# Decoder layer on one core: the splits of the experts' weights, all placed in front of the last routing

## The chip, the cores and the metric

One core of a Trainium2 chip runs the whole program in one launch. The metric is the device time of one execution in microseconds (us); less is better. The engines are TensorE (PE), VectorE (DVE), ScalarE (ACT), GpSimd (POOL) and SyncE (SP), which only issues transfers here.

## The reference

x has 8 sequences of 256 tokens with 512 channels, in float32. Three blocks follow one another, each behind a layer norm and added to its input:

```python
x = x + _L0_attn_ref(_layernorm(x), w_qkv, w_out)          # causal self attention, 16 heads of 32
x = x + _L0_xattn_ref(_layernorm(x), mask, ctx, ctx, wq, wk, wv, wo)
                                    # one head of 512; keys and values: 256 rows of ctx, and 256 made from x
x = x + _L0_ffn_ref(_layernorm(x), wg, W, b)
...
logits = xt @ wg                                           # 8 experts
probs = softmax(logits); idx = argmax(probs); gate = probs[idx]
out = onehot(idx) * gate applied to (einsum('nh,eoh->neo', xt, W) + b)
```

Each token goes to its best expert alone, a 512 x 512 matrix with a bias, and the result is weighted with its probability.

## The kernel before

The program has three stages, each a block of its own with one instruction stream for each engine; at the end of a block the engines meet (line 946 is that of the second block). `self_attention` is the first stage. `cross_attention` is the second, and `mixture_of_experts` the third. Tokens are worked on in batches of 256 (B = 8), as two tiles of 128.

**Split products.** Every float32 product is made of three passes over rounded halves (`three_pass`, L60): a matrix is kept as a high part (rounded to float32r) and a low part (the rest). For activations ACT writes the high part (L1120) and DVE subtracts it from the source to get the low part (L1281).

**The experts' weights** are split in the same way, by `ExpertWeights` (L900 to L929). All eight stay in `w_hi` and `w_lo` of [128, 4, 8 x 512]; a matrix is 128 partitions x 2048 columns, 1 MB. The steps of one expert e are: `load` (SP) brings it into one of three staging buffers, e modulo 3, once the expert that was there has been split; `high` (ACT, L918) copies it rounded; `low` (GpSimd or DVE, L923) subtracts, over all 2048 columns in one instruction. Before the experts move in, the same places of `w_hi` and `w_lo` hold the weights and working matrices of the cross attention: q, k and v in the places of experts 0, 1 and 2, keys in 3, xt and qt in 4, values in 5, wo in 6, pt and ot in 7. An expert can be split only when its place is no longer in use: 0 to 2 once the q, k and v products of the last batch are done (v1 of batch 6), the others during or behind the last batch.

**The second stage** works through jobs, in one order on all engines:

```python
ORDER = ("X0 X1 s0 s1 q0 q1 p0 p1 q2 q3 o0 o1 o2 o3 k0 y0 y1 k1 k2 k3 v0 Y0 Y1 v1 l0 l1").split()
```

X transposes the normed tokens, q, k, v make queries, keys and values, s the scores, p transposes the probabilities, o multiplies with the values, y with wo, Y transposes the tokens normed for the third stage, l makes the logits. q, k, v and X are made a batch ahead, so the last batch runs only LAST: s0 s1 p0 p1 o0 to o3 y0 y1 Y0 Y1 l0 l1. Behind y1, DVE takes the statistics of x2 (L1256, L1260, b_veps in L1262), GpSimd raises to the power -1/2 (`rstd_ln3`, L1085), DVE writes xn_sb (L1266), TensorE transposes it (Y), DVE copies to xt3 (L1314), TensorE makes logits (L1237), DVE copies them (L1318).

**The routing** of a batch is done while the next one runs; that of the last batch stands at the head of the third stage. `choose` (DVE, L831 to L847: r_lmax, r_diff, r_eq, r_best, r_onehot, and the gate, with the exponential on ACT, L851), `count` (TensorE, L857 to L860), `place_tokens` (DVE, L869 to L877). Then `store_entries` (GpSimd, L884) scatters token numbers and gates into the table `slots` in memory, two indirect transfers of 128 entries, and `next_tokens` (GpSimd, L890, L893) waits until they have landed and writes the next token numbers, for which the next `choose` waits.

GpSimd's end of the second stage reads, before: `rstd_ln3(6)`, `store_entries(5)`, `next_tokens(5)`, lows of experts 1 and 2, `store_entries(6)`, low of 4, `rstd_ln3(7)`, `next_tokens(6)`. DVE makes the low part of 0 ahead of the last batch and that of 3 behind o3. ACT makes the high parts 0, 1, 2 ahead of the last batch and 3, 4, 5 behind it. In the third stage GpSimd makes the low part of 5 behind the last `store_entries`, ACT the high parts of 6 and 7, and DVE their low parts, ahead of its first product. The bias (16 KB, broadcast to 128 partitions, 2 MB) goes into `bias_sb`, whose first half holds wo raw until wo has been split.

**The third stage** takes 23 blocks of 128 tokens sorted by expert: SP reads 128 entries of `slots`, GpSimd gathers the rows (into the staging buffers, once the last expert of each has been split), TensorE transposes and multiplies (L1556, L60), DVE adds bias and residual, GpSimd scatters the result. TensorE starts when all experts are split and the owners of the blocks are known; c_at_i (L1613) is what SP needs to find a block's entries.

Of the kernel before, what the change touches and what calls it, by code (L numbers as in the profile page):

```python
# [10 lines left out]
F32 = mybir.dt.float32  # L11
# [9 lines left out]
P = 128  # L21
# [7 lines left out]
E = 8  # L29
# [866 lines left out]
class ExpertWeights:  # L896
# [1 line left out]

    def __init__(self, nc, cx, stage, loaded):
        sb = lambda n: cx.enter_context(nc.sbuf_tensor(n, [P, DC, E * D], F32R))
        sem = lambda n: cx.enter_context(nc.semaphore("e_" + n))
        self.hi, self.lo, self.stage, self.loaded = sb("w_hi"), sb("w_lo"), stage, loaded
        self.hi_done = sem("hi_done")
        self.split = [sem(f"split{i}") for i in range(STAGED)]

    def place(self, e, start=0, stop=D):
        return [t[:, :, e * D + start:e * D + stop] for t in (self.hi, self.lo)]

    def load(self, sp, w, e):
        wait(sp, self.split[e % STAGED], e // STAGED)
        sp.dma_start(self.stage[e % STAGED][:], w[e].rearrange("(c p) n -> p c n", p=P))\
            .then_inc(self.loaded[e % STAGED], 16)

    def high(self, nc, act, e):
        act.wait_ge(self.loaded[e % STAGED], 16 * (e // STAGED + 1))
        nc.scalar.copy(self.place(e)[0], self.stage[e % STAGED][:]).then_inc(self.hi_done, 1)  # L918

    def low(self, engine, e):  # L920
        hi, lo = self.place(e)
        engine.wait_ge(self.hi_done, e + 1)
        engine.tensor_tensor(lo, self.stage[e % STAGED][:], hi.bitcast(F32), ALU.subtract)\  # L923
            .then_inc(self.split[e % STAGED], 1)

    def all_split(self, engine):
        for i in range(STAGED):
            engine.wait_ge(self.split[i], len(range(i, E, STAGED)))


def cross_attention(nc, ident, routing, x1, x1_out, x1_last_out, ctx, ctx_t, wo, wg,
# [14 lines left out]
    with ExitStack() as cx:  # L946
# [78 lines left out]
        @block.sync  # L1025
        def _(sp):
            chunks = lambda t: t.rearrange("(c p) n -> p c n", p=P)
            channels = lambda b: ctx_t[b * D:(b + 1) * D, :] if isinstance(b, int) else ctx_t[bass.ds(b * D, D), :]
            load_ctx_t = lambda b: sp.dma_start(cin_t[:], chunks(channels(b))).then_inc(ct_in, 16)
            sp.wait_ge(unused_done, 2)  # L1030
            sp.dma_start(routing.table.rearrange("(p k) c -> p k c", p=P), unused[:]).then_inc(init_in, 16)
            load_ctx_t(1)
            sp.dma_start(wo_raw, chunks(wo)).then_inc(wo_in, 16)
            sp.dma_start(cin[:], batch_rows(ctx, 1)).then_inc(c_in, 16)
            sp.wait_ge(x1_out, 16 * (B - 1))
            sp.dma_start(xin[:], batch_rows(x1, 2)).then_inc(x_in, 16)
# [3 lines left out]
            for i in range(STAGED):  # L1040
                experts.load(sp, w, i)

            sp.wait_ge(wo_split, 2)
            sp.dma_start(bias_sb[:], bass.AP(tensor=bias.tensor, offset=bias.offset, ap=[[0, P], [1, E * D]]))\
                .then_inc(bias_in, 16)

            def batch(n, more, load):

                if load:
                    if not (isinstance(n, int) and n == 0):  # L1050
                        sp.wait_ge(xn_ready, n * TB)
                        sp.dma_start(xin[:], batch_rows(x1, n + 2)).then_inc(x_in, 16)
                    sp.wait_ge(ct_split, n + 1)
                    load_ctx_t(n + 2)
                    sp.wait_ge(c_split, n + 1)
                    sp.dma_start(cin[:], batch_rows(ctx, n + 2)).then_inc(c_in, 16)
                if not more:
                    for e in range(STAGED, E - 1):
                        experts.load(sp, w, e)
                sp.wait_ge(job_ev, ev_at("y1", n))  # L1060
                sp.dma_start(batch_rows(x2n[:, 0:D], n), x2_sb[:]).then_inc(x2_out, 16)
                if more:
                    sp.dma_start(xr[:], batch_rows(x1, n + 1)).then_inc(xr_in, 16)
                sp.wait_ge(xn3_ready, (n + 1) * TB)
                sp.dma_start(batch_rows(x2n[:, D:], n), xn3_sb[:]).then_inc(xn3_out, 16)

            batch(0, True, True)
            with sp.Fori(1, B - 2) as n:
                batch(n, True, True)
            batch(B - 2, True, False)  # L1070
            batch(B - 1, False, False)
            experts.load(sp, w, E - 1)

        @block.gpsimd
        def _(pool):
# [28 lines left out]
                routing.next_tokens(nc, pool, tick_pool, n - 1)  # L1104
            rstd_ln3(B - 2)
            routing.store_entries(nc, pool, tick_pool, B - 3)
            routing.next_tokens(nc, pool, tick_pool, B - 3)
            for e in (1, 2):
                experts.low(nc.gpsimd, e)
            routing.store_entries(nc, pool, tick_pool, B - 2)  # L1110
            experts.low(nc.gpsimd, 4)
            rstd_ln3(B - 1)
            routing.next_tokens(nc, pool, tick_pool, B - 2)

        @block.scalar
        def _(act):
# [15 lines left out]
            def batch(n):  # L1132
                for j in order(n):
                    if j[0] == "s":
                        q = int(j[1])
                        act.wait_ge(mx_done, n * TB + q + 1)
                        nc.scalar.activation(prob[:, q, :], bank(j, n)[:, :], ACT.Exp, scale=scale,
                                             bias=nmax[:, q:q + 1], accum_out=rsum[:, q:q + 1]).then_inc(ex_done, 1)
                    if j == "s1" and order(n) is ORDER:
                        ctx_t_hi(n + 1)  # L1140
                    if j in hi_jobs(order(n)):
                        hi_part(j, n)
                    if j == route_after(n) and has_routing(n):
# [9 lines left out]
            for e in range(STAGED):  # L1153
                experts.high(nc, act, e)
            batch(B - 1)
            for e in (3, 4, 5):
                experts.high(nc, act, e)

        @block.tensor
        def _(pe):  # L1160
# [87 lines left out]
                batch(n)  # L1248
            batch(B - 1)

        @block.vector
        def _(dve):
            def norm_stats(which, k, src, done):
# [39 lines left out]
            def batch(n):  # L1293
                for j in order(n):
# [33 lines left out]
                        ctx_t_lo(n + 1)  # L1328
                    if j == "o3" and order(n) is ORDER:
                        ctx_lo(n + 1)  # L1330
                    if j == "o3" and order(n) is LAST:
                        experts.low(nc.vector, 3)
                    if j == "p1":
                        nc.vector.reciprocal(rinv[:], rsum[:]).then_inc(rinv_done, 1)
                    if j == "y1":
# [20 lines left out]
def mixture_of_experts(nc, ident, routing, x2n, x2n_out, w, bias_sb, bias_in, out, stage, experts):  # L1356
# [17 lines left out]
    with ExitStack() as cx:  # L1374
# [35 lines left out]
        def rows(k, columns):  # L1410


            place, part = divmod(k % RX, RX // STAGED)
            first_column = part * 2 * D
            return stage[(E + place) % STAGED][:].rearrange("p c n -> p (c n)")[:, first_column + columns.start:
                                                                               first_column + columns.stop]


# [43 lines left out]
        def _(pool):  # L1462
# [9 lines left out]
            nc.gpsimd.tensor_copy(first[:], first_i[:]).then_inc(consts, 1)  # L1472
            nc.gpsimd.memset(at[:], 0.0).then_inc(consts, 1)
            routing.store_entries(nc, pool, tick_pool, B - 1)
            experts.low(nc.gpsimd, 5)
            for s in x2n_out:
                pool.wait_ge(s, 16 * B)

            def gather(i, k):

                m = number_of(i, k)
                if isinstance(i, int) and k < RX and k % (RX // STAGED) == 0:

                    place = (E + k // (RX // STAGED)) % STAGED
                    pool.wait_ge(experts.split[place], len(range(place, E, STAGED)))
# [31 lines left out]
        @block.scalar  # L1517
        def _(act):
            routing.exponentials(nc, act, B - 1)
            for e in (6, 7):  # L1520
                experts.high(nc, act, e)

            def gather_numbers(i, k):
                act.wait_ge(tab_in[k % RX], (turn(i, k) + 1) * 16)
# [58 lines left out]
        def _(dve):  # L1583
# [64 lines left out]
def program(nc, x, ctx, ctx_t, w_qkv, w_out, wq, wk, wv, wo, wg, w, bias, out):  # L1648
    with ExitStack() as cx:
# [11 lines left out]
        loaded = [sem(f"expert_in{i}") for i in range(STAGED)]  # L1661
        experts = ExpertWeights(nc, cx, stage, loaded)
# [3 lines left out]
        bias_sb, bias_in = cx.enter_context(nc.sbuf_tensor("bias_sb", [P, E * D], F32)), sem("bias_in")  # L1666
        x2_sb, xn3_sb = rows_tensor("x2_sb"), rows_tensor("xn3_sb")
        cross_attention(nc, ident, routing, x1, x1_out, x1_last_out, ctx, ctx_t, wo, wg,
                        x2n, x2n_out, xin, xr, xn, x2_sb, xn3_sb, bias, bias_sb, bias_in, stage, w, experts)
# [24 lines left out]
```

## Time and profile before

| what | us |
|---|---|
| median of 3 runs (lowest to highest) | 764.4 (761.05 to 765.31) |
| the profiled execution's own time | 764.43 |
| its span | 762.7 |
| PE busy | 677.9 (89%) |
| DVE busy | 497.5 (65%) |
| POOL busy | 322.2 (42%) |
| ACT busy | 309.2 (41%) |

Times of the trace are counted from the span's start. The last batch of the second stage runs from about 613 to 651.6, the third stage from there to the end. TensorE's granted clock over the span is 0.957 of full.

### The profile page before, as it was taken

Reading aid. Unit: us, or ns where it says so; the run is one execution under the profiler, and the core shown is the slowest. Engines: PE = TensorE matmul, PEld = TensorE weight load, DVE = VectorE, ACT = ScalarE, POOL = GpSimd, SP = SyncE. Lnnn points to the kernel's source line nnn. Section 1 sums busy time; section 2 is a strip of 40 time slices with the busy share of each in tenths; the row PEclk is TensorE's granted clock in tenths of the full one; section 3 lists DMA queues with packets and bytes.
Section 4 is the critical chain, followed back from the end, with each engine's and each line's share of the span. In section 5 each row is a group of like instructions: output and inputs, shape, how many; then the busy total and the mean of one; then the engine's idle time right before and its main releaser. Section 6 shows DMA issues by size and latency. Waiting matters only on the chain. (4 is left out here: it accounts for less than half of the span.)

```text
span 762.7 us, 18978 instructions
## 1 busy us (share of the span) xinstructions
PE 677.9 (89%) x6040; PEld 604.5 (79%) x6041; DVE 497.5 (65%) x1452; ACT 309.2 (41%) x986; POOL 322.2 (42%) x542
## 2 busy tenths in 40 slices
PE   4758999999999999999999999999999985159995
PEld 4748798989888878878898989899999974148884
DVE  4767788888787878846565555555554556716663
ACT  3545566656655666723131313131313143112220
POOL 4376757575756787714001010101010145436652
PEclk9969999999999999999999999999999988559998
DMA  6477875656656657719905252534230345156530
GB/s 247 140 158 117 129 145 111 152 129 127 145 116 142 138 111 136 180 40 314 328 29 114 52 123 42 115 50 125 40 110 0 83 137 144 50 154 194 190 113 13
DMA packets 142888, 95.09 MB, mean 125 GB/s; under 512 B 110846, under 2 KB 115070, under 8 KB 142720
## 3 DMA queue, kind: packets, MB, share of 16 engines
q1 hardware_dynamic: 137184, 82.00, 45.5%
q0 software_dynamic: 5664, 12.61, 5.5%
q8 instruction: 19, 0.31, 0.2%
q14 instruction: 21, 0.17, 0.1%
HBM read 56.14 MB, written 18.77 MB: 98 GB/s over the span
## 5 line engine op out<-in xcount | busy, mean ns | idle before, releaser
L508 ACT ACTIVATE prob<-prob,shift 128x128 f32<-128x128 f32 (+1 forms) x256 | 114.6, 449 | 117.2 <-POOL shift L419 116.7
L1120 ACT CAST w_hi<-b_bank 128x256 fp32r<-128x256 f32 (+1 forms) x132 | 56.3, 444 | 157.5 <-PE b_bank L60 138.8
L60 PE MATMUL b_bank<-w_hi 128*128 128x256 f32 (+1 forms) x536 | 109.7, 327 | 3.2 <-DVE w_lo L1281 3.2
L60 PE MATMUL a_job<-w_hi 128*128 128x256 f32 (+1 forms) x488 | 94.5, 317 | 15.0 <-DVE w_lo L711 7.2
L60 PE MATMUL b_bank<-w_hi,w_lo 128*128 128x256 f32 (+1 forms) x536 | 106.8, 322 | 0.0
L60 PE MATMUL b_bank<-w_lo,w_hi 128*128 128x256 f32 (+1 forms) x536 | 106.7, 322 | 0.0
L732 DVE CUSTOM_DVE_ANT_0 prob<-a_s,mask 128x128 f32<-128x128 f32 (+1 forms) x256 | 79.7, 348 | 29.3 <-PE a_s L608 29.2
L1281 DVE TENSOR_TENSOR w_lo<-b_bank,w_hi 128x256 fp32r<-128x256 f32 (+1 forms) x132 | 63.0, 508 | 52.3 <-ACT w_hi L1120 51.7
L60 PEld LDWEIGHTS a_job<-w_hi 128*128 128x128 f32 x488 | 71.3, 195 | 24.8 <-DVE w_lo L711 7.8
L60 PEld LDWEIGHTS b_bank<-w_hi 128*128 128x128 f32 x536 | 82.4, 192 | 9.9 <-DVE w_lo L1281 2.5
L60 PEld LDWEIGHTS b_bank<-w_lo,w_hi 128*128 128x128 f32 x536 | 83.9, 192 | 7.5
L60 PEld LDWEIGHTS b_bank<-w_hi,w_lo 128*128 128x128 f32 x536 | 83.9, 193 | 7.3
L740 DVE TENSOR_TENSOR p_part<-prob,p_part 128x384 f16<-128x384 f32 x128 | 78.4, 612 | 15.0 <-POOL p_part L426 13.4
L60 PE MATMUL a_job<-w_lo,w_hi 128*128 128x256 f32 (+1 forms) x488 | 87.7, 303 | 0.0
L60 PE MATMUL a_job<-w_hi,w_lo 128*128 128x256 f32 (+1 forms) x488 | 87.1, 301 | 0.0
L419 POOL TENSOR_SCALAR shift<-nmax 128x2 f32<-128x2 f32 x128 | 44.3, 346 | 84.1 <-DVE nmax L732 79.6
L60 PEld LDWEIGHTS a_job<-w_lo,w_hi 128*128 128x128 f32 x488 | 72.3, 195 | 3.0
L60 PEld LDWEIGHTS a_job<-w_hi,w_lo 128*128 128x128 f32 x488 | 72.2, 195 | 2.9
L426 POOL CAST p_part<-prob 128x384 f16<-128x384 f32 x128 | 64.3, 503 | 14.3 <-DMA pt<-p_part 5.6
L711 DVE TENSOR_TENSOR w_lo<-a_job,w_hi 128x256 fp32r<-128x256 f32 (+1 forms) x92 | 43.2, 477 | 18.8 <-ACT w_hi L495 18.4
L1085 POOL TENSOR_TENSOR b_rstd<-b_veps,b_expo 128x2 f32<-128x2 f32 x8 | 5.6, 697 | 103.6 <-DVE b_veps L1262 103.5
L508 ACT ACTIVATION_READ_ACCUMULATOR prob<-prob,shift 128x1 f32 x256 | 48.1, 188 | 0.0
(160 smaller groups left out, 1132.3 us busy)
## 6 DMA issues: line engine op xcount, KB each, us to landing
stage<-in_w SPq DMA_DIRECT2D x8, 1024.0 KB, 6.0
xin<-in_x SPq DMA_DIRECT2D x8, 512.0 KB, 4.4
xr<-in_x SPq DMA_DIRECT2D x8, 512.0 KB, 3.9
x<-xr SPq DMA_DIRECT2D x8, 512.0 KB, 3.2
xin<-x SPq DMA_DIRECT2D x8, 512.0 KB, 8.7
xr<-x SPq DMA_DIRECT2D x8, 512.0 KB
x2n<-x_sb SPq DMA_DIRECT2D x8, 512.0 KB
x2n<-xn_sb SPq DMA_DIRECT2D x8, 512.0 KB, 7.2
```

The costliest lines, as they stand in the source:

```text
L60: ins = pe_matmul(out, a, b, start=first and i == 0, stop=last and i == len(steps) - 1)
L419: nc.gpsimd.tensor_scalar(shift[:, e, :], nmax[:, e, :], LN_UNIT, None, ALU.add).then_inc(shift_done, 1)
L426: nc.gpsimd.tensor_copy(p_part[:, t % NPROB, 0, :], prob[:, t % NPROB, :]).then_inc(p_hi_done, 1)
L508: a = nc.scalar.activation(prob[:, e % NPROB, cols], prob[:, e % NPROB, cols], ACT.Exp, scale=-1.0, bias=shift[:, e, q:q + 1], accum_out=r ...
L711: nc.vector.tensor_tensor(lo, src, hi, ALU.subtract).then_inc(job_ev, 1)
L732: m = nc.vector.tensor_tensor_reduce(out=prob[:, s % NPROB, cols], in0=s_ps[s % HG][:, q, 0:P * (q + 1)], in1=mask[:, P * (1 - q):], scale ...
L740: nc.vector.tensor_tensor(p_part[:, t % NPROB, 1, :], prob[:, t % NPROB, :], p_part[:, t % NPROB, 0, :], ALU.subtract).then_inc(p_done, 1)
L1085: nc.gpsimd.tensor_tensor(rstd[:, 1, :], veps[:, 1, :], expo[:], ALU.pow).then_inc(ln3_rstd, 1)
L1120: nc.scalar.copy(hi, src).then_inc(job_hi, 1)
L1281: nc.vector.tensor_tensor(lo, src, hi.bitcast(F32), ALU.subtract).then_inc(job_ev, 1)
```

## The change

The experts are no longer staged in three buffers taken in turn but in five: the three staging buffers and two halves of `bias_sb`, in the order 0 1 2 3 4 0 1 2. Expert 4 is loaded with 0, 1 and 2 at the head of the second stage, expert 3 once wo has been split (it takes wo's half). In the last batch SP loads 5, 6 and 7, and then the bias, once 3 and 4 are split; only then does it store x2 and xn3 of the last batch. The low parts are made in four instructions of 512 columns each, on both engines. Who makes which, and when:

- ACT: high parts 0, 1, 2 as before; 3 and 4 behind p1's high part and ahead of the exponentials; 5 behind o3's; 6 and 7 once y1 is done on TensorE.
- GpSimd: low 1 between `store_entries(5)` and `next_tokens(5)`, then 2 and 4; after `store_entries(6)` half of 5; after `rstd_ln3(7)` the other half of 5 and all of 6; then `next_tokens(6)`.
- DVE: low 0 ahead of the last batch; of 3 one piece behind each of o0 to o3; of 7 two pieces behind Y1, one behind l0 and one behind l1.

In the third stage no split is left, and the gathers wait for the splits of 5, 6 and 7 by the new numbering.

```diff
 class ExpertWeights:
+    BUFFER = (0, 1, 2, 3, 4, 0, 1, 2)
...
+    def add_stages(self, bias_sb):
+        self.stage += [bias_sb[:, i * DC * D:(i + 1) * DC * D].rearrange("p (c n) -> p c n", c=DC) for i in range(2)]
...
+    def earlier(self, e):
+        return self.BUFFER[:e].count(self.BUFFER[e])
+
     def load(self, sp, w, e):
-        wait(sp, self.split[e % STAGED], e // STAGED)
-        sp.dma_start(self.stage[e % STAGED][:], w[e].rearrange("(c p) n -> p c n", p=P))\
-            .then_inc(self.loaded[e % STAGED], 16)
+        b = self.BUFFER[e]
+        wait(sp, self.split[b], self.earlier(e) * DC)
+        sp.dma_start(self.stage[b], w[e].rearrange("(c p) n -> p c n", p=P)).then_inc(self.loaded[b], 16)
...
-    def low(self, engine, e):
+    def low(self, engine, e, pieces=range(DC)):
         hi, lo = self.place(e)
+        b = self.BUFFER[e]
         engine.wait_ge(self.hi_done, e + 1)
-        engine.tensor_tensor(lo, self.stage[e % STAGED][:], hi.bitcast(F32), ALU.subtract)\
-            .then_inc(self.split[e % STAGED], 1)
+        for c in pieces:
+            engine.tensor_tensor(lo[:, c, :], self.stage[b][:, c, :], hi[:, c, :].bitcast(F32), ALU.subtract)\
+                .then_inc(self.split[b], 1)
+
+    def wait_split(self, engine, e):
+        engine.wait_ge(self.split[self.BUFFER[e]], DC * (self.earlier(e) + 1))
...
 # second stage, SP
-            for i in range(STAGED):
-                experts.load(sp, w, i)
-
+            for e in (0, 1, 2, 4):
+                experts.load(sp, w, e)
             sp.wait_ge(wo_split, 2)
-            sp.dma_start(bias_sb[:], bass.AP(tensor=bias.tensor, offset=bias.offset, ap=[[0, P], [1, E * D]]))\
-                .then_inc(bias_in, 16)
+            experts.load(sp, w, 3)
...
                 if not more:
-                    for e in range(STAGED, E - 1):
+                    for e in (5, 6, 7):
                         experts.load(sp, w, e)
+                    for e in (3, 4):
+                        experts.wait_split(sp, e)
+                    sp.dma_start(bias_sb[:], bass.AP(tensor=bias.tensor, offset=bias.offset, ap=[[0, P], [1, E * D]]))\
+                        .then_inc(bias_in, 16)
                 sp.wait_ge(job_ev, ev_at("y1", n))
...
-            experts.load(sp, w, E - 1)
 # second stage, GpSimd
             rstd_ln3(B - 2)
             routing.store_entries(nc, pool, tick_pool, B - 3)
+            experts.low(nc.gpsimd, 1)
             routing.next_tokens(nc, pool, tick_pool, B - 3)
-            for e in (1, 2):
+            for e in (2, 4):
                 experts.low(nc.gpsimd, e)
             routing.store_entries(nc, pool, tick_pool, B - 2)
-            experts.low(nc.gpsimd, 4)
+            experts.low(nc.gpsimd, 5, (0, 1))
             rstd_ln3(B - 1)
+            experts.low(nc.gpsimd, 5, (2, 3))
+            experts.low(nc.gpsimd, 6)
             routing.next_tokens(nc, pool, tick_pool, B - 2)
 # second stage, ACT
+                    for e in {"p1": (3, 4), "o3": (5,)}.get(j, ()) if order(n) is LAST else ():
+                        experts.high(nc, act, e)
                     if j == route_after(n) and has_routing(n):
                         routing.exponentials(nc, act, n - 1)
...
             batch(B - 1)
-            for e in (3, 4, 5):
+            act.wait_ge(job_done, done_at("y1", B - 1))
+            for e in (6, 7):
                 experts.high(nc, act, e)
 # second stage, DVE
+        LOWS = {"o0": (3, (0,)), "o1": (3, (1,)), "o2": (3, (2,)), "o3": (3, (3,)), "Y1": (7, (0, 1)), "l0": (7, (2,)),
+                "l1": (7, (3,))}
...
-                    if j == "o3" and order(n) is LAST:
-                        experts.low(nc.vector, 3)
+                    if order(n) is LAST and j in LOWS:
+                        experts.low(nc.vector, *LOWS[j])
 # third stage
             routing.store_entries(nc, pool, tick_pool, B - 1)
-            experts.low(nc.gpsimd, 5)
...
             routing.exponentials(nc, act, B - 1)
-            for e in (6, 7):
-                experts.high(nc, act, e)
...
-            for e in (6, 7):
-                experts.low(nc.vector, e)
             dve.wait_ge(bias_in, 16)
```

## Rows read from the trace of the kernel before

**Rows 1.** The chain of waits, in order of time: start, length, what

```profile
651.65 0.18 DVE r_lmax L831
651.85 0.17 DVE r_diff L833
...
656.29 9.03 DMA slots<-r_entry,r_slot_i
```

**Rows 2.** Timeline, DVE and GpSimd at the last two scatters (start, length, operation)

```profile
634.09 2.29 DVE L923 TENSOR_TENSOR w_lo<-stage,w_hi 128x2048 fp32r<-128x2048 f32 x1 [0.60 <-ACT w_hi L918]
634.29 3.02 POOL L884 DMA_INDIRECT slots<-r_entry,r_slot_i  x1 [8.34 <-DVE r_slot_i L877]
...
656.29 0.96 POOL L884 DMA_INDIRECT slots<-r_entry,r_slot_i  x1 [0.30 <-issue]
656.67 5.16 DVE L1613 SCALAR_TENSOR_TENSOR c_at_i<-c_block_no,c_at_sum 128x27 int32<-128x27 f32 x1
657.27 4.51 POOL L923 TENSOR_TENSOR w_lo<-stage,w_hi 128x2048 fp32r<-128x2048 f32 x1
```

**Rows 3.** Timeline of TensorE, the last batch: o0, o2, y0, the end of y1

```profile
623.28 1.19 PE L60 MATMUL b_bank<-w_hi 128*128 128x256 f32 x4 [1.61 <-DVE w_lo L1281]
...
628.74 0.72 PE L60 MATMUL b_bank<-w_hi 128*128 128x256 f32 x4
...
632.87 1.17 PE L60 MATMUL b_bank<-w_hi 128*128 128x512 f32 x4 [1.01 <-DVE w_lo L1281]
...
637.50 1.07 PE L60 MATMUL b_bank<-w_hi,w_lo 128*128 128x512 f32 x4
```

**Rows 4.** Busy time by stretch: us, PE, PEld, DVE, ACT, POOL, then TensorE's granted clock

```profile
624.00:628.00 4.00, 4.00 (x21) 4.00 (x20) 3.22 (x9) 0.57 (x2) 1.96 (x1) 0.50 0.61 233
```

**Rows 5.** Timeline of DVE, the last batch

```profile
623.29 2.70 DVE L833 TENSOR_TENSOR r_diff<-r_logits,r_lmax 128x16 f32<-128x16 f32 x1
...
626.95 0.40 DVE L1281 TENSOR_TENSOR w_lo<-b_bank,w_hi 128x256 fp32r<-128x256 f32 x1
...
641.17 1.98 DVE L1262 TENSOR_SCALAR b_veps<-b_mv 128x2 f32<-128x2 f32 x1
644.06 1.00 DVE L1266 TENSOR_SCALAR xn_sb<-x_sb,b_mv,b_rstd 128x512 f32<-128x512 f32 x2 [0.91 <-POOL b_rstd L1085]
...
646.73 0.69 DVE L1314 COPY b_xt<-b_bank 128x512 f32<-128x512 f32 x1 [0.16 <-PE b_bank L1190]
```

**Rows 6.** Timeline of GpSimd, the last batch

```profile
616.92 9.04 POOL L923 TENSOR_TENSOR w_lo<-stage,w_hi 128x2048 fp32r<-128x2048 f32 x2
...
638.61 4.51 POOL L923 TENSOR_TENSOR w_lo<-stage,w_hi 128x2048 fp32r<-128x2048 f32 x1
643.23 0.72 POOL L1085 TENSOR_TENSOR b_rstd<-b_veps,b_expo 128x2 f32<-128x2 f32 x1
...
647.16 0.18 POOL L893 CAST r_entry<-r_token 128x2 int32<-128x2 f32 x1 [0.17 <-POOL r_token L890]
```

**Rows 7.** Timeline, GpSimd and DVE in the first stage, two places

```profile
252.04 0.40 POOL L434 COPY rinv_wide<-rinv 128x256 f32<-128x256 f32 x1
252.40 1.29 POOL L191 TENSOR_TENSOR w_lo<-stage,w_hi 128x512 fp32r<-128x512 f32 x1
252.75 0.98 DVE L687 TENSOR_SCALAR a_veps<-a_mv 128x2 f32<-128x2 f32 x1
...
261.06 0.50 POOL L426 CAST p_part<-prob 128x384 f16<-128x384 f32 x1
261.18 0.67 DVE L691 TENSOR_SCALAR xn<-xin,a_mv,a_rstd 128x512 f32<-128x512 f32 x1
...
261.51 0.59 POOL L434 COPY rinv_wide<-rinv 128x256 f32<-128x256 f32 x1
```

**Rows 8.** Transfers by line: issuing queue, count, KB each, us to landing

```profile
bias_sb<-in_bias SPq DMA_DIRECT2D x1, 2048.0 KB, 10.2
```

**Rows 9.** Timeline of ScalarE, the high parts of experts 0 to 2

```profile
611.86 5.52 ACT L918 CAST w_hi<-stage 128x2048 fp32r<-128x2048 f32 x3
```

More of the change, by code:

```diff
@@ L896, with __init__ @@
 class ExpertWeights:
-    def __init__(self, nc, cx, stage, loaded):
+    BUFFER = (0, 1, 2, 3, 4, 0, 1, 2)
+    def __init__(self, nc, cx, stage):
         sb = lambda n: cx.enter_context(nc.sbuf_tensor(n, [P, DC, E * D], F32R))
         sem = lambda n: cx.enter_context(nc.semaphore("e_" + n))
-        self.hi, self.lo, self.stage, self.loaded = sb("w_hi"), sb("w_lo"), stage, loaded
+        self.hi, self.lo, self.stage = sb("w_hi"), sb("w_lo"), [t[:] for t in stage]
         self.hi_done = sem("hi_done")
-        self.split = [sem(f"split{i}") for i in range(STAGED)]
+        self.loaded = [sem(f"in{i}") for i in range(max(self.BUFFER) + 1)]
+        self.split = [sem(f"split{i}") for i in range(max(self.BUFFER) + 1)]
@@ L916, in high @@
     def high(self, nc, act, e):
-        act.wait_ge(self.loaded[e % STAGED], 16 * (e // STAGED + 1))
-        nc.scalar.copy(self.place(e)[0], self.stage[e % STAGED][:]).then_inc(self.hi_done, 1)
-    def low(self, engine, e):
+        act.wait_ge(self.loaded[self.BUFFER[e]], 16 * (self.earlier(e) + 1))
+        nc.scalar.copy(self.place(e)[0], self.stage[self.BUFFER[e]]).then_inc(self.hi_done, 1)
+    def low(self, engine, e, pieces=range(DC)):
         hi, lo = self.place(e)
+        b = self.BUFFER[e]
@@ L922, in low @@
         engine.wait_ge(self.hi_done, e + 1)
-        engine.tensor_tensor(lo, self.stage[e % STAGED][:], hi.bitcast(F32), ALU.subtract)\
-            .then_inc(self.split[e % STAGED], 1)
+        for c in pieces:
[3 more added lines that the diff above has]
+        engine.wait_ge(self.split[self.BUFFER[e]], DC * (self.earlier(e) + 1))
     def all_split(self, engine):
-        for i in range(STAGED):
-            engine.wait_ge(self.split[i], len(range(i, E, STAGED)))
+        for e in range(E - len(self.split), E):
+            self.wait_split(engine, e)
@@ L1039, in _ @@
             sp.dma_start(wg_sb[:], chunks(wg)).then_inc(wg_in, 16)
-            for i in range(STAGED):
-                experts.load(sp, w, i)
+            for e in (0, 1, 2, 4):
+                experts.load(sp, w, e)
             sp.wait_ge(wo_split, 2)
-            sp.dma_start(bias_sb[:], bass.AP(tensor=bias.tensor, offset=bias.offset, ap=[[0, P], [1, E * D]]))\
-                .then_inc(bias_in, 16)
+            experts.load(sp, w, 3)
             def batch(n, more, load):
@@ L1414, in rows @@
             first_column = part * 2 * D
-            return stage[(E + place) % STAGED][:].rearrange("p c n -> p (c n)")[:, first_column + columns.start:
+            return stage[place][:].rearrange("p c n -> p (c n)")[:, first_column + columns.start:
                                                                                first_column + columns.stop]
@@ L1482, in gather @@
                 if isinstance(i, int) and k < RX and k % (RX // STAGED) == 0:
-                    place = (E + k // (RX // STAGED)) % STAGED
-                    pool.wait_ge(experts.split[place], len(range(place, E, STAGED)))
+                    experts.wait_split(pool, E - STAGED + k // (RX // STAGED))
                 if isinstance(i, int) and k < AHEAD:
@@ L1660, in program @@
         stage_in = [sem(f"stage_in{i}") for i in range(STAGED)]
-        loaded = [sem(f"expert_in{i}") for i in range(STAGED)]
-        experts = ExpertWeights(nc, cx, stage, loaded)
+        experts = ExpertWeights(nc, cx, stage)
         self_attention(nc, ident, x, w_qkv, w_out, x1, xin, xr, xn, x1_out, x1_last_out, stage, stage_in, (wq, wk, wv),
@@ L1666, in program @@
         bias_sb, bias_in = cx.enter_context(nc.sbuf_tensor("bias_sb", [P, E * D], F32)), sem("bias_in")
+        experts.add_stages(bias_sb)
         x2_sb, xn3_sb = rows_tensor("x2_sb"), rows_tensor("xn3_sb")
```

## The prediction

> **What bounds the kernel now.** I read the chain of waits first. Its last part starts at the routing of the last batch: the block of the second stage ends, r_lmax runs at 651.65, and from there eleven small steps lead to the two scatters into slots, the later of which is on the chain from 656.29 for 9.03, until 665.32 [rows 1]. Then come the table, the gathers and 23 blocks of products. No split of an expert is on that chain. What the change takes out of this tail is GpSimd's 4.51 (expert 5) and DVE's two of 2.29 (6 and 7, right behind expert 5), and c_at_i, which took 5.16 because it ran into GpSimd's split: it ended at 661.83, with 3.5 to spare before 665.32 [rows 1, 2]. So the tail gives nothing back by this reading; it starts when the block ends.
>
> Next the timelines of the last batch, where the change puts this work. TensorE: o0 starts at 623.28 at half clock (granted 0.50 from 624 to 628), o2 at 628.74 at full, y0 waits 1.01 for the low part of o3 and starts at 632.87, and y1 ends at 638.57 [rows 3, 4]. Two of DVE's operations there are long: r_diff 2.70, which ended with GpSimd's pair of splits (616.92 + 9.04 = 625.96), and b_veps 1.98, which ended at 643.15, when GpSimd's split of expert 4 (638.61 + 4.51) had ended [rows 5, 6]. The last batch's r_diff, with GpSimd idle, takes 0.17 [rows 1]. Only b_veps is on the path: rstd, xn_sb, Y, l and the end of the block follow it.
>
> **How the two engines meet.** A GpSimd piece of 512 columns took 1.29 in the first stage, and DVE's a_veps, issued inside it, took 0.98 and ended with it; a whole 2048 takes 4.51, so a row of pieces should step by about 1.24 (two points on a line: 0.2 fixed) [rows 6, 7]. For the turn-taking there is one place: between two GpSimd operations DVE's xn (0.67) got in, and the second GpSimd operation grew from 0.40 to 0.59 [rows 7]. So I let them alternate: each DVE operation with two SBUF operands, or a tensor_scalar of more than one column, waits for the running GpSimd piece and then goes before the next. A DVE piece of 512 is a quarter of 2.29 and its start, 0.65.
>
> **The change part by part, in the old trace's times.**
> (a) Loads: e4 goes into the bias's half early, e3 follows wo's split, the bias (10.2 to land, off anyone's path until 683) is read when e3 and e4 are split, near 637 [rows 8]. The bytes in front of batch 0 are the same 5 MB. The x2 store queues behind the bias, but its first reader is the gather near 669. Cost 0. If that cover went, at most 10.2.
> (b) ACT: highs 0 to 2 stay (three in 5.52) [rows 9]. Two more, 1.84 each, follow p1's high part at 622.3 and end at 626.0; r_ex and o0's high part then run at 626.1 to 626.3, as they do now (DVE's row after them is at 626.95) [rows 5]. Cost 0.1. Highs 5, 6, 7 are covered.
> (c) GpSimd: low(1) starts at 615.7 beside DVE's low(0), ends near 621.3, next_tokens takes 0.6 [rows 6], low(2) runs from 621.9, low(4) right behind it. Eight pieces of 1.24 are 9.9; with DVE in between it holds the port until about 634, where now it is free from 625.96 to 634.29. DVE meets it in choose: r_diff waits for one piece (1.1 instead of 2.5), but the second r_eq, the ranking and onehot meet a piece each. onehot then ends near 628.9 (the counting on TensorE wants it at 628.5) and o0's low part starts near 629.2 instead of 626.95.
> (d) DVE's e3 pieces after o0, o1, o2: each meets a piece of low(4): o0's low part to 629.6, piece to 630.7, o1's to 631.1, piece to 632.6, o2's to 633.0, piece to 634.5, o3's to 634.9. y0 starts at 635.1 instead of 632.87: **+2.2**. From below: if DVE never waits it needs 0.42 + 0.61 for a job of 1.44, and y0 moves by 0.1. From above: if GpSimd always goes first, it is free at 632 and DVE has r_diff to o3's low part still to do, about 5.5: y0 at 637.7, +4.8.
> (e) b_veps: GpSimd has done only half of e5 by then (stores from 636.7, two pieces to 641.6; b_veps at 643.4). It costs 0.17 instead of 1.98: **-1.8**.
> (f) Behind rstd GpSimd's queue now holds six pieces (half of e5, e6) and next_tokens, 6 x 1.24 + 0.6 = 8.0. rstd ended at 643.95 and r_lmax started at 651.65, 7.7 later [rows 1, 6]. Between these pieces must go DVE's two xn_sb (0.5 each) and at least three of the four e7 pieces (0.65 each), together 3.0, and the barrier needs 0.3: 8.0 + 3.0 + 0.3 + 0.1 = 11.4 against 7.7, **+3.7**. DVE's own order gives the same: xn_sb ends late by 1.3 to 2.7, Y1's copy at 648.9 to 650.2 instead of 647.42, its last e7 piece near 655.4, r_lmax at 655.7 instead of 651.65 [rows 1, 5]. From below: with no meetings the queue gives 8.0 + 0.3, +0.6 at most.
> Sum: 2.2 - 1.8 + 3.7 = +4.1, less 0.1 for rounding. The profiled execution took 764.43 with a span of 762.7, and the median of the runs is 764.4, so it goes on either: 768.4. By the lower bounds: 0.1 - 1.8 + 0.6 = -1.1, 763.3. By the upper: 4.8 - 1.8 + 3.7 = 6.7, 771.1.
>
> **Rivals.**
> 1. The clock falls again. TensorE's wait ahead of y0 grows from 1.0 to 3.2. o0 and o1 took 5.26 at half clock (623.28 to 628.54), o2 and o3 about 2.95 at full [rows 3]: a fall there would cost y0 and y1 about 2.3 more. For it: the clock fell in this trace after waits of 2.0 and 1.6 ahead of o0. Against it: the wait of 1.0 ahead of y0 did nothing, and 3.2 stands between. 770.7.
> 2. The meetings cost little: DVE gets the port in gaps that I don't see, or holds it over several short operations. Then (d) is 0.1 to 1, (f) 0.6 to 2: 763.3 to 765.6, say 764.6, no difference.
> 3. The other side: the scatter lands sooner. Its 9.03 are the longest piece of the tail, and right behind its issue run GpSimd's split and DVE's c_at_i and splits, all of which go [rows 1, 2]. If its descriptors waited for the 4.51, the time would be 768.4 - 4.5 = 763.9, and with the cheap meetings of rival 2 764.6 - 4.5 = 760.1. It decides for faster only from a saving of 3.8 beyond what the meetings cost. Against it: where a scatter was held up, GpSimd's own row grew (3.02 beside DVE's split of 2.29); the last one took its plain 0.96, ahead of the split [rows 2].
> The Trainium skill (SBUF — State Buffer, the box on the "DVE blocks DMA" trap in the section on two separate sides) says that a GpSimd-issued DMA can seem blocked because GpSimd cannot write its descriptors while DVE holds the shared port. It would put the loss in the landing time and make rival 3 likelier; by that rule alone the time would be near 760. The rows of the trace put the loss in the issuing row, so I leave this rival small.
> 4. GpSimd always wins the port, next_tokens is late, and choose waits for its token as well: (d) at its upper bound, with a fall of the clock 773.
>
> **How the numbers follow.** The forecast (alternating turns, clock as now, 766.5 to 770.5) has 0.45, rival 1 0.17, rival 2 0.24, rival 3 0.07, rival 4 0.07. About 0.5%, 3.8 here, is what a measurement can tell from no change: the line lies at 768.2, just under the forecast. Faster (below 760.6) needs rival 3 with rival 2's terms: 0.05. Slower: half and a little of the forecast, nearly all of rivals 1 and 4: 0.49. Same: 0.46. The range leaves out the far part of rivals 3 and 4: 763.3 to 771.5.
>
> **What the profile after would show.** Right: y0 near 635 with its wait behind a low part of o3; DVE rows of its e3 pieces of 1.3 to 1.9 instead of 0.69; b_veps 0.17; long xn_sb and e7 pieces; r_lmax near 655.7, and the same distance from there to the first product; c_at_i near 0.4 with no effect. Wrong: pieces of 0.7 beside a running GpSimd piece (no meetings), r_lmax at or before 652, or a scatter on the chain for under 6. The forecast also fails if the early loads move batch 0, which I cost at nothing.

## The result, and the profile after

The changed kernel takes 765.37 us (median of 20 runs, 763.33 to 768.97) against 761.62 (20 runs, 760.03 to 765.31) for the kernel before: a ratio of 1.0047, 95% interval 1.0037 to 1.0057, so about 3.6 us slower (2.8 to 4.3). 768.4 was forecast, with a range of 763.3 to 771.5. The forecast started from the first median of before, 764.4, and was +4.0 against it. The measured time lies 3.0 below 768.4, and 2.8 of these come from that starting point (764.4 against 761.62). What the forecast says of the change itself is +4.0, against a measured +3.6. Slow executions are left out of all ratios; there was one among the 12 of after_again (1345.74 us) and one among the 10 of bias_last (1133.38).

A warning comes first. The trace of before belongs to an execution of 764.43, which is slower than nearly all of its 20; that of after belongs to the fastest of 20, 763.33. Laid side by side they show a faster kernel. So I read in each trace distances between events of one execution, and leave the times to the medians.

DVE's timeline of the changed kernel, last batch (start, length, operation), compares with [rows 5]. L934 is the line of `low`, so its rows are the pieces of the low parts:

```profile
623.02 0.91 DVE L833 TENSOR_TENSOR r_diff<-r_logits,r_lmax 128x16 f32<-128x16 f32 x1
623.85 0.16 DVE L834 TENSOR_TENSOR r_eq<-r_logits,r_lmax 128x16 f32<-128x16 f32 x1
624.05 1.15 DVE L837 TENSOR_TENSOR r_eq<-r_eq,r_rank 128x16 f32<-128x16 f32 x1
625.23 0.17 DVE L840 TENSOR_REDUCE r_best<-r_eq 128x2 f32<-128x16 f32 x1
625.43 1.00 DVE L842 TENSOR_TENSOR r_onehot<-r_eq,r_best 128x16 bf16<-128x16 f32 x1
...
627.02 1.19 DVE L934 TENSOR_TENSOR w_lo<-bias_sb,w_hi 128x512 fp32r<-128x512 f32 x1
...
628.47 1.45 DVE L934 TENSOR_TENSOR w_lo<-bias_sb,w_hi 128x512 fp32r<-128x512 f32 x1
...
640.40 0.17 DVE L1288 TENSOR_SCALAR b_veps<-b_mv 128x2 f32<-128x2 f32 x1
641.48 2.81 DVE L1292 TENSOR_SCALAR xn_sb<-x_sb,b_mv,b_rstd 128x512 f32<-128x512 f32 x2 [0.91 <-POOL b_rstd L1100]
...
646.17 2.69 DVE L934 TENSOR_TENSOR w_lo<-stage,w_hi 128x512 fp32r<-128x512 f32 x2
...
648.85 1.68 DVE L934 TENSOR_TENSOR w_lo<-stage,w_hi 128x512 fp32r<-128x512 f32 x1
...
652.78 0.17 DVE L831 TENSOR_REDUCE r_lmax<-r_logits 128x2 f32<-128x16 f32 x1 [1.57 <-PEq L960]
```

GpSimd's timeline of the same compares with [rows 6]:

```profile
621.39 5.01 POOL L934 TENSOR_TENSOR w_lo<-stage,w_hi 128x512 fp32r<-128x512 f32 x4
626.37 6.38 POOL L934 TENSOR_TENSOR w_lo<-bias_sb,w_hi 128x512 fp32r<-128x512 f32 x4
...
640.64 0.72 POOL L1100 TENSOR_TENSOR b_rstd<-b_veps,b_expo 128x2 f32<-128x2 f32 x1 [1.72 <-DVE b_veps L1288]
641.35 8.64 POOL L934 TENSOR_TENSOR w_lo<-stage,w_hi 128x512 fp32r<-128x512 f32 x6
649.95 0.66 POOL L890 TENSOR_SCALAR r_token<-r_token 128x2 f32<-128x2 f32 x1
650.78 0.47 POOL L893 CAST r_entry<-r_token 128x2 int32<-128x2 f32 x1 [0.17 <-POOL r_token L890]
652.74 0.15 POOL L1489 MEMSET c_upto<- 128x64 f32 x1 [1.49 <-POOLq L960]
```

Four things are to be seen. The two engines meet: of choose's four small two-operand steps, which take 0.17 to 0.24 alone, three take 0.91 to 1.15 and one (L834) gets by with 0.16; a piece of 0.69 takes 1.19 to 1.45, and xn_sb's pair 2.81 instead of 1.00. b_veps is back at 0.17. GpSimd's row of six pieces follows rstd at once. And r_lmax starts 11.42 behind the end of rstd (641.36), where it was 7.70 [rows 1, 6]. TensorE's row ahead of y0 compares with [rows 3], and the scatter in the chain of waits (start, length, what) with [rows 1]:

```profile
632.08 1.17 PE L60 MATMUL b_bank<-w_hi 128*128 128x512 f32 x4 [1.53 <-DVE w_lo L1307]
```

```profile
657.42 8.85 DMA slots<-r_entry,r_slot_i
```

The scatter took 8.85 instead of 9.03, and c_at_i 0.19 instead of 5.16; from r_lmax to the first product it is 25.8, against 26.7.

TensorE's clock differs between the two traces. In before all six rows of o0 and o1 ran at half clock. In after it rose during the fourth, and o0 and o1 took 4.3 instead of 5.3. The fifth of these six rows on TensorE's timeline, in before and then in after:

```profile
626.83 1.05 PE L60 MATMUL b_bank<-w_lo,w_hi 128*128 128x256 f32 x4
```

```profile
626.34 0.64 PE L60 MATMUL b_bank<-w_lo,w_hi 128*128 128x256 f32 x4
```

Below, p0 is TensorE's first transposition of the probabilities, at 620.61 in the trace of before and 620.34 in that of after.

### The profile page after: what moved, and what is told of

Its sections match the earlier page's. It is cut to its first block and busy times, and to the rows that moved or that the text cites. A ratio compares the mean times of both kernels' runs of the same rounds, so it can differ in the third digit from the quotient of the medians.

```text
span 761.6 us, 19005 instructions
## 1 busy us (share of the span) xinstructions
PE 677.4 (89%) x6040; PEld 603.9 (79%) x6041; DVE 495.1 (65%) x1460; ACT 309.2 (41%) x986; POOL 330.3 (43%) x558
```

## The experiments

Ratios are to the kernel before, run beside each on the same chip, with 95% intervals, from 12 executions of each variant (20 of after, 10 of bias_last, 4 of e6_twice and of whole). Every variant does all of the program's work. Two distances are read from every trace: p0 to y0 (steps (c) and (d), and TensorE's clock in o0 to o3), and the end of rstd to r_lmax (step (f)).

| run | ratio | p0 to y0 | y0 to end of y1 | rstd to r_lmax |
|---|---|---|---|---|
| before (trace ahead of the prediction) | 1 | 12.3 | 5.7 | 7.70 |
| before_again | one execution, 761.3 us | 12.1 | 5.7 | 7.71 |
| after | 1.0047 | 11.7 | 5.7 | 11.42 |
| after_again | 1.0036 (1.0018 to 1.0053) | 12.9 | 7.3 | 11.41 |
| both_late | 0.9990 (0.9975 to 1.0005) | 13.1 | 7.3 | 7.70 |
| pool_late | 0.9989 (0.9973 to 1.0005) | 12.9 | 5.7 | 8.30 |
| dve_late | 1.0030 (1.0014 to 1.0046) | 12.9 | 5.7 | 9.79 |
| b_e4_late | 1.0009 (0.9996 to 1.0022) | 12.1 | 5.7 | 7.87 |
| quiet | 0.9980 (0.9965 to 0.9995) | 12.1 | 5.7 | 7.71 |
| bias_last | 1.0045 (1.0024 to 1.0065) | 12.9 | 7.3 | 11.4 |
| e6_twice | 1.0111 (1.0088 to 1.0134) | 12.3 | 5.7 | 16.47 |
| e3_behind | 1.0027 (1.0016 to 1.0039) | 12.3 | 5.7 | 11.41 |
| whole | 1.0112 (1.0083 to 1.0140) | 16.7 | 5.7 | 14.0 |

**both_late.** The splits behind rstd go back to the third stage, on both engines.

```diff
 # changed kernel, GpSimd, second stage
             rstd_ln3(B - 1)
-            experts.low(nc.gpsimd, 5, (2, 3))
-            experts.low(nc.gpsimd, 6)
             routing.next_tokens(nc, pool, tick_pool, B - 2)
 # third stage, behind store_entries(B - 1)
+            experts.low(nc.gpsimd, 5, (2, 3))
+            experts.low(nc.gpsimd, 6)
 # DVE: no entries Y1, l0, l1 in LOWS; third stage
+            experts.low(nc.vector, 7)
             dve.wait_ge(bias_in, 16)
```

> The changed kernel, but the second half of expert 5 and all of 6 (GpSimd) and all four pieces of expert 7 (DVE) stand in the third stage, behind the last scatter. Theory A (the queue of six GpSimd pieces and three or four DVE pieces between rstd and the block's end costs 3.7, b_veps gives 1.8): r_lmax starts about 7.7 after rstd ends, as before, instead of 11.4; the time is 3.7 below the changed kernel, about 0 to 1.8 below the kernel before (ratio to before 0.998 to 1.000). Rival B (the measured loss of 3.6 comes from elsewhere: the clock falling ahead of y0, the early loads, or the x2 stores queued behind the bias): ratio to before stays near 1.004 to 1.005.

Measured: 0.9990, and 7.70 as before. The loss of 0.0047 is gone, so what stands behind rstd is needed for it; the loads and the clock alone don't make it. The clock fell in this very trace (y0 and y1 took 7.3).

**pool_late.** Of that edit only GpSimd's half.

> The changed kernel, but only GpSimd's six pieces (half of expert 5, and 6) are moved behind the last scatter; DVE keeps expert 7 behind Y1, l0 and l1. Theory A: DVE's pieces are back at 0.65 each, xn_sb's pair back at 1.0, and only the last piece (0.65) lies on the path: r_lmax about 8.3 after rstd; 3.0 below the changed kernel, ratio to before 0.998 to 1.001. Theory A2 (it is DVE's own four pieces that cost, not GpSimd's queue): only about 1 is won, ratio 1.003 to 1.004. Rival B: ratio near 1.0045.

Measured: 0.9989 and 8.30 (8.3 was expected). With GpSimd idle, DVE's pieces are short again, in DVE's timeline:

```profile
642.33 1.00 DVE L1290 TENSOR_SCALAR xn_sb<-x_sb,b_mv,b_rstd 128x512 f32<-128x512 f32 x2 [0.91 <-POOL b_rstd L1100]
...
645.61 1.28 DVE L934 TENSOR_TENSOR w_lo<-stage,w_hi 128x512 fp32r<-128x512 f32 x2
```

Of DVE's pieces only the last, behind l1, is on the path. A2, that DVE's own pieces cost most, falls. By its ratio this kernel lies 4.4 us below the changed one, by the distance 3.1; the rest is within what the two intervals leave open.

**dve_late.** Of that edit only DVE's half.

> The changed kernel, but only DVE's four pieces of expert 7 are moved to the third stage; GpSimd keeps its six pieces behind rstd. Theory A: the queue is 6 x 1.25 + 0.6 and the two xn_sb in between, 9.4 from rstd to r_lmax instead of 11.4: 2.0 below the changed kernel, ratio to before 1.001 to 1.003. Theory A2: nearly all of the 3.7 is won, ratio 0.998 to 1.000. Rival B: near 1.0045.

Measured: 1.0030 and 9.79 (9.4 was expected). GpSimd's timeline:

```profile
641.43 7.74 POOL L934 TENSOR_TENSOR w_lo<-stage,w_hi 128x512 fp32r<-128x512 f32 x6
...
651.20 0.15 POOL L1488 MEMSET c_upto<- 128x64 f32 x1 [1.49 <-POOLq L960]
```

Without DVE's four pieces the row is 0.90 shorter and next_tokens' two operations are 0.73 shorter (0.57 from the start of the first to the end of the second, against 1.30); r_lmax comes 1.63 sooner. The third stage begins 1.5 after GpSimd's last operation; the step of 0.3 that I had put in for the block's end is what follows where DVE is last.

**e6_twice.** Four more pieces in GpSimd's row: the low part of 6 is made twice.

```diff
 # changed kernel, GpSimd, second stage
             experts.low(nc.gpsimd, 5, (2, 3))
+            pool.wait_ge(experts.hi_done, 7)
+            hi, lo = experts.place(6)
+            for c in range(DC):
+                nc.gpsimd.tensor_tensor(lo[:, c, :], experts.stage[1][:, c, :], hi[:, c, :].bitcast(F32), ALU.subtract)\
+                    .then_inc(extra, 1)
+            pool.wait_ge(extra, DC)
             experts.low(nc.gpsimd, 6)
```

> The changed kernel, in which GpSimd makes the low part of expert 6 twice: four more pieces of 512 columns between rstd and the block's end (a waste, the result is the same). Theory A (GpSimd's queue sets the block's end): each piece adds 1.25, r_lmax comes 5.0 later, 16.4 behind rstd; ratio to before 1.0047 + 0.0065 = 1.011. Rival (DVE's order or the logits set it): under 2 is added, ratio under 1.0075.

Measured: 1.0111 and 16.47 (16.4 was expected). DVE is done at 652.23 there and waits, as its timeline shows:

```profile
650.56 1.67 DVE L934 TENSOR_TENSOR w_lo<-stage,w_hi 128x512 fp32r<-128x512 f32 x1
657.86 0.17 DVE L831 TENSOR_REDUCE r_lmax<-r_logits 128x2 f32<-128x16 f32 x1 [5.63 <-PEq L960]
```

So GpSimd's queue sets the end of the block. r_lmax comes 5.05 later, 1.26 for each added piece. In its parts that is again a sum: the row grew by 5.8 (ten pieces end 14.4 behind rstd, six ended 8.6 behind), and next_tokens, which met no piece of DVE here, was 0.7 shorter.

**b_e4_late.** The gain of step (e) alone, on the kernel before: the low part of 4 goes to the third stage.

```diff
 # kernel before, GpSimd
             routing.store_entries(nc, pool, tick_pool, B - 2)
-            experts.low(nc.gpsimd, 4)
 # third stage
+            experts.low(nc.gpsimd, 4)
             experts.low(nc.gpsimd, 5)
 # SP: the load of 7 moves to the head of the third stage
```

> The kernel before, but GpSimd's low part of expert 4 is made in the third stage, ahead of that of expert 5 (and the load of 7, which waits for it, too). This is the gain of step (e) alone: b_veps is back at 0.17, Y, l and the block's end come 1.8 earlier. The splits then end near 671 instead of 667, still ahead of the first gather's landing at 677. Theory A: ratio to before 0.9976, 1.8 us. Rival: the block's end is set by something else behind b_veps (the token scatter landing for next_tokens at 646.8), or the tail absorbs it: ratio 1.000.

Measured: 1.0009, and the expectation failed, though the step did what it was to do: b_veps took 0.17, and r_lmax came 11.4 behind the end of y1 instead of 13.1. (The 7.87 from rstd, instead of 7.70, come from next_tokens, which waited for its scatter and was the last to end.) The tail gave it back. DVE, GpSimd and SyncE in one timeline of the third stage:

```profile
654.15 9.60 DVE L1613 SCALAR_TENSOR_TENSOR c_at_i<-c_block_no,c_at_sum 128x27 int32<-128x27 f32 x1
654.74 8.95 POOL L923 TENSOR_TENSOR w_lo<-stage,w_hi 128x2048 fp32r<-128x2048 f32 x2
...
664.81 14.84 SPq L1446 DMA_DIRECT2D c_tab<-slots  x13
...
668.84 2.29 DVE L923 TENSOR_TENSOR w_lo<-stage,w_hi 128x2048 fp32r<-128x2048 f32 x1 [2.39 <-ACT w_hi L918]
669.44 1.73 POOL L1488 CAST c_gather_no<-c_tab 128x1 uint32<-128x1 int32 x1
```

c_at_i did not go in between GpSimd's two instructions (one row, x2) but lasted until both were done. It ended at 663.75 and became the step that SP's first read waits for; then the second gather's number (normally 0.20) waited for DVE's split of 7. From r_lmax (649.12) to the first product (677.38) it is 28.3, against 25.8 and 26.7 in the two traces of the kernel before.

**e3_behind.** DVE's four pieces of expert 3 all behind o3, the rest as in the changed kernel.

```diff
-        LOWS = {"o0": (3, (0,)), "o1": (3, (1,)), "o2": (3, (2,)), "o3": (3, (3,)), "Y1": (7, (0, 1)), "l0": (7, (2,)),
+        LOWS = {"o3": (3, range(DC)), "Y1": (7, (0, 1)), "l0": (7, (2,)),
```

> The changed kernel with DVE's four pieces of expert 3 all behind o3, instead of one behind each of o0 to o3. Theory A (these pieces, each waiting for one of GpSimd's, make the low parts of o1 to o3 late, and the longer wait ahead of y0 lets the clock fall in some executions): p0 to y0 is 12.1 to 12.3 again instead of 12.9, no fall of the clock in y0 and y1; 0.8 to 1.2 below the changed kernel, ratio to before 1.003. Rival (the choose of batch 6, whose four two-operand steps wait for a piece each, is what delays o0's low part, and with it all of o): p0 to y0 stays at 12.9 and the ratio at 1.0045.

Measured: 1.0027, p0 to y0 12.3, and the wait ahead of y0 back at 1.01, on TensorE's timeline:

```profile
631.51 1.17 PE L60 MATMUL b_bank<-w_hi 128*128 128x512 f32 x4 [1.01 <-DVE w_lo L1307]
```

All four choosing steps met a piece here (0.92, 1.32, 1.21, 1.00), and o0's low part started 7.6 behind p0 instead of 6.3, and yet y0 was hardly late. So the meetings of choose alone are hidden. The pieces between o0 and o3 alone are hidden too, which e6_twice shows: it has them, but choose met only three pieces, o0's low part started at 6.4, and y0 came at 12.3 with its wait of 1.01. In the five traces with both (after_again, both_late, pool_late, dve_late, bias_last) o0's low part starts 7.6 to 7.8 behind p0, DVE is late with every low part from there on, and y0 comes at 12.9 to 13.1. L834 and o0's low part on DVE's timeline, of after_again and then of e6_twice:

```profile
622.36 1.32 DVE L834 TENSOR_TENSOR r_eq<-r_logits,r_lmax 128x16 f32<-128x16 f32 x1
...
626.42 0.40 DVE L1307 TENSOR_TENSOR w_lo<-b_bank,w_hi 128x256 fp32r<-128x256 f32 x1
```

```profile
623.30 0.16 DVE L834 TENSOR_TENSOR r_eq<-r_logits,r_lmax 128x16 f32<-128x16 f32 x1
...
626.15 0.41 DVE L1314 TENSOR_TENSOR w_lo<-b_bank,w_hi 128x256 fp32r<-128x256 f32 x1
```

p0 is at 618.85 and 619.79. After is like e6_twice in this, and its y0 came at 11.7 since TensorE's clock rose early in o1.

**after_again.** The changed kernel, a second trace. **before_again.** The kernel before, likewise.

> The changed kernel itself once more, on the chip of its neighbours here, for a second trace. Both theories: ratio to before 1.0037 to 1.0057. Theory A: rstd to r_lmax 11.4 again, p0 to y0 12.9 rather than the 11.7 of the first trace, since the first trace was of the fastest execution of 20. Rival (the first trace is typical): p0 to y0 11.7 again.

> The kernel before once more, for a second trace: p0 to the end of y1 17.8 to 18.0, b_veps 1.98, rstd to r_lmax 7.7, by every theory; it shows how far one execution of it lies from another in the parts that the change does not touch (the scatter's landing, the first product's clock).

after_again gave 1.0036. Its trace shows rival 1: a longer wait ahead of y0, and y0 and y1 partly at half clock. Its rows of TensorE's timeline, and of the busy time by stretch (columns as in [rows 4]; the last two are the DMA engines' busy share and GB/s):

```profile
631.78 1.17 PE L60 MATMUL b_bank<-w_hi 128*128 128x512 f32 x4 [1.83 <-DVE w_lo L1307]
```

```profile
628.00:632.00 4.00, 2.17 (x18) 2.00 (x17) 3.96 (x8) 2.39 (x3) 2.75 (x2) 1.00 0.42 162
632.00:636.00 4.00, 4.00 (x12) 3.15 (x12) 0.93 (x3) 0.16 (x1) 2.47 (x3) 0.60 0.56 193
```

The granted clock is 1.00 in the stretch with the wait and 0.60 in the next. y0 and y1 took 7.3 instead of 5.7. This happened in three of the seven traces with pieces of expert 3 beside GpSimd's of expert 4 (after_again, both_late and bias_last, with waits of 1.8, 2.0 and 1.9 ahead of y0). The four without a fall had waits of 1.0, 1.4, 1.5 and 1.7. The six other traces all had a wait of 1.0 there, and none shows a fall in y0 and y1. before_again repeats [rows 5, 6]: b_veps 1.98, 7.71 behind rstd.

**bias_last.** The bias is loaded behind the x2 and xn3 stores of the last batch.

> The changed kernel with the bias loaded behind both stores of the last batch instead of ahead of them. Theory A: nothing waits for these stores before the first gather, the ratio to before stays at 1.0037 to 1.0057. Rival (the 2 MB of bias hold up the x2 and xn3 stores or the scatters, and this is part of the loss): 1 to 3 is won, ratio 1.001 to 1.003.

Measured: 1.0045 (1.0024 to 1.0065), no different from the changed kernel's 1.0047. The queue order costs nothing that can be seen, as step (a) had it; the interval would hide up to 1.7 us.

**whole.** One instruction in place of pieces that stand together.

```diff
-        for c in pieces:
-            engine.tensor_tensor(lo[:, c, :], self.stage[b][:, c, :], hi[:, c, :].bitcast(F32), ALU.subtract)\
-                .then_inc(self.split[b], 1)
+        first, last = pieces[0], pieces[-1] + 1
+        engine.tensor_tensor(lo[:, first:last, :], self.stage[b][:, first:last, :],
+                             hi[:, first:last, :].bitcast(F32), ALU.subtract).then_inc(self.split[b], last - first)
```

> The changed kernel with the low parts made in one instruction wherever the pieces stand together (GpSimd's experts 1, 2, 4, 6 in one of 2048 columns, 5 in two of 1024, DVE's 0 in one, the pieces of 3 and 7 as they are). Theory A (turns are taken instruction by instruction): a step of choose can now wait 4.5 for expert 4, o0's low part comes near 631, y0 2 to 3 later, xn_sb's second half waits for all of expert 6; 3 to 5 above the changed kernel, ratio to before 1.009 to 1.011. Rival (it is the sum of GpSimd's work that counts, not the size of its instructions): within 1 of the changed kernel, ratio 1.003 to 1.006.

Measured: 1.0112. The same work costs 5 more, and the meetings show why: each lasts up to a whole instruction. TensorE's and DVE's timelines:

```profile
630.82 0.19 PE L857 MATMUL r_ranks<-r_onehot,r_before 128*128 128x8 bf16 x1 [3.08 <-DVE r_onehot L842]
```

```profile
626.34 4.42 DVE L842 TENSOR_TENSOR r_onehot<-r_eq,r_best 128x16 bf16<-128x16 f32 x1
...
646.85 7.13 DVE L1292 TENSOR_SCALAR xn_sb<-x_sb,b_mv,b_rstd 128x512 f32<-128x512 f32 x2 [0.91 <-POOL b_rstd L1100]
```

Here TensorE itself stands: the counting between o1 and o2 waits for r_onehot, and its last transpositions wait for xn_sb's second half, which waited for all of expert 6. TensorE's wait of 3.08 was followed by half clock through o2 and o3 (1.05 a row instead of 0.64), which is part of the 16.7.

**quiet.** The version that follows from the first four runs.

```diff
 # changed kernel, GpSimd
-            for e in (2, 4):
-                experts.low(nc.gpsimd, e)
+            experts.low(nc.gpsimd, 2)
             routing.store_entries(nc, pool, tick_pool, B - 2)
-            experts.low(nc.gpsimd, 5, (0, 1))
+            experts.low(nc.gpsimd, 4)
             rstd_ln3(B - 1)
-            experts.low(nc.gpsimd, 5, (2, 3))
-            experts.low(nc.gpsimd, 6)
 # third stage, behind store_entries(B - 1)
+            pool.wait_ge(at_done, 1)
+            experts.low(nc.gpsimd, 5)
+            experts.low(nc.gpsimd, 6)
 # DVE: no entry l1 in LOWS; third stage
+            experts.low(nc.vector, 7, (3,))
             dve.wait_ge(bias_in, 16)
```

> A version put together from what the first four runs showed. GpSimd: expert 4 behind the scatter of batch 6 (not beside o0 to o3), all of 5 and 6 behind the last scatter and a wait for c_at_i; DVE: expert 7's last piece in the third stage, the other three behind Y1 and l0. Theory A (meetings beside o0 to o3 delay y0 by 0.8, the queue behind rstd costs 3.7, b_veps gives 1.8): y0 starts about 12.1 behind the start of p0, as in the kernel before, instead of 12.9; r_lmax 7.7 behind rstd; c_at_i takes 0.2; 1.8 faster than the kernel before, ratio 0.9976 (0.9965 to 0.9990). Rival: expert 4's four pieces run into b_veps, which then waits up to 1.2, or the splits in the tail hold up the first gathers: ratio 0.999 to 1.001.

Measured: 0.9980 (0.9965 to 0.9995), 1.5 us faster than the kernel before. DVE's timeline, with GpSimd idle beside o0 to o3, b_veps waiting for the end of a piece only, and a new long row in the tail:

```profile
627.61 0.68 DVE L934 TENSOR_TENSOR w_lo<-bias_sb,w_hi 128x512 fp32r<-128x512 f32 x1
...
640.94 0.48 DVE L1284 TENSOR_SCALAR b_veps<-b_mv 128x2 f32<-128x2 f32 x1
...
655.46 9.92 DVE L1636 TENSOR_SCALAR c_owner_i<-c_owner 128x27 int32<-128x27 f32 x1
```

c_owner_i is done at 665.4, ahead of the first gathered rows, and costs nothing. GpSimd's row of eight pieces has nothing to spare, though: it ends at 665.33, just when the first block's entries must have come (SP issued their read at 663.50, and it takes 1.7 in the other traces' chains), and in this trace the chain of waits runs through it and no longer through the scatter. On GpSimd's timeline:

```profile
655.54 9.79 POOL L934 TENSOR_TENSOR w_lo<-stage,w_hi 128x512 fp32r<-128x512 f32 x8
665.36 0.66 POOL L1511 CAST c_gather_no<-c_tab 128x1 uint32<-128x1 int32 x1
```

## Why the prediction was right

**The tail gives nothing back: right to within half a microsecond.** From r_lmax to the first product the changed kernel takes 25.8 and 25.5 in its two traces, the kernel before 26.7 and 25.8. c_at_i is short, and what follows the scatter comes hardly sooner. b_e4_late shows the other side of it: c_at_i has some 3.5 to spare, and once it uses more it is on the path.

**Step (a): right.** From the first transposition of the second stage to s0 of the last batch both first traces take 268.5 (344.38 to 612.88, and 344.12 to 612.62), so the early loads cost nothing; bias_last shows no cost of the bias's place either.

**Steps (c) and (d), +2.2: mis-sized.** The meetings are there, but too long in the forecast. Behind p0, it had o0's low part start at 8.6, o3's end at 14.3, low(4) end at 13.4 and y0 start at 14.5. In after_again these are 7.6, 12.8, 11.9 and 12.9, and in after o0's low part starts at 6.4 and low(4) ends at 12.4. So choose was over-priced by 1.0 to 2.2: it met a piece three times or four, and some of the pieces were half over. The steps from o0 to o3 were over-priced by 0.5. p0 to y0 took 12.7 on average over the seven traces that have these pieces (11.7 to 13.1), against 12.2: +0.5, and +0.8 in the five in which choose met four pieces. e3_behind and e6_twice show that it takes both, four meetings in choose and the pieces between o0 and o3.

**Rival 1, the fall of the clock, belongs into the forecast and not beside it.** It had a chance of 0.17 and a price of 2.3; it came in three traces of seven at 1.6, which is +0.7 in the mean of so few.

**Step (e), -1.8: right.** rstd follows the end of y1 by 3.6 instead of 5.4.

**Step (f), +3.7: right in its sum, 11.42 against 11.4, and wrong in its parts.** The forecast had 7.4 for six pieces, 3.0 of meetings, 0.6 for next_tokens, and 0.3 for the block's end. It was 8.64 for the pieces, so 1.2 of meetings, then 1.26 for next_tokens, which met DVE's pieces as well, and 1.5 to the next block. That 1.8 too much and 1.9 too little cancel is luck; that the queue sets the step is not. That GpSimd's queue is what counts is shown from both sides, by pool_late (-3.1), dve_late (-1.6) and e6_twice (+5.1).

The sum of the measured terms is 0.5 + 0.7 - 1.8 + 3.7 = +3.1, against a measured +3.6 (2.8 to 4.3); the difference stays open, within the interval. both_late agrees: without (f) it is -0.6 by this sum and -0.8 by its ratio.

**Rival 3: did not happen.** The scatter took 8.00 to 8.85 in the seven traces with no split right behind it (after, after_again, bias_last, dve_late, e3_behind, e6_twice, whole), and 8.44 to 9.03 in the four with one (before, before_again, both_late, pool_late): 0.3 less on average, where the rival needed 4.5. Rival 2 and rival 4 did not happen either; whole shows what long waits like those of rival 4 cost.

## What to carry to other kernels

Before moving background work forward, look at what closes the stage: here all engines met at the block's end, and a queue on a little-used engine, six pieces behind its last urgent operation, became the path. In these traces work in pieces cost the other engine up to one piece per meeting, so keep such rows away from chains of many small two-operand steps, and away from any operation whose result a queue waits for. A delay that is hidden alone may show together with a second one, as the two beside o0 to o3 did; take out each by itself before calling one harmless. And compare distances inside traces, not two traces' ends: the two here differed in the wrong direction.

## What was not expected of the hardware

**Who takes turns.** DVE's choosing steps, its pieces and xn_sb went in after one piece of GpSimd's row. c_at_i and c_owner_i did not: they lasted until two whole instructions were done (9.60 in b_e4_late), six pieces (8.01 in both_late) and eight (9.92 in quiet). c_owner_i has one operand and started 0.08 before the first piece, c_at_i 0.62 before it in both_late. DVE's row and GpSimd's, from both_late:

```profile
656.67 8.01 DVE L1634 SCALAR_TENSOR_TENSOR c_at_i<-c_block_no,c_at_sum 128x27 int32<-128x27 f32 x1
```

```profile
657.29 7.35 POOL L934 TENSOR_TENSOR w_lo<-stage,w_hi 128x512 fp32r<-128x512 f32 x6
```

Both write whole numbers, 27 columns of them, and both started while GpSimd was issuing a scatter. In after and dve_late c_at_i started during such an issue too, with no split behind it, and took 0.19. Which of these things matters was not tried.

**The end of a block.** Where GpSimd is last, its first operation of the next block comes 1.49 behind (seven traces, after and b_e4_late among them). Where DVE is last, r_lmax comes 0.32 behind it (before).

**The clock.** The granted clock fell in y0 and y1 in the three executions whose waits ahead of y0 were 1.8 to 2.0, and in none of the ten whose waits were 1.0 to 1.7. The fall cost 1.6 over y0 and y1. Thirteen traces don't show that the wait alone decides.
